# Path attention on one core: where the transposed inverses lie, how much of a level is multiplied, and when the softmax of a batch is done

## The reference, cut to what matters

```python
Mw  = where(strict, einsum('bhtd,bhsd->bhts', wh, wh) * beta, 0)
rhs = where(strict, einsum('bhtd,bhjd->bhtj', wh, kh) * beta, 0)
Bmat = solve_triangular(Mw + eye(t), rhs, lower=True)
qw  = where(incl, einsum('bhid,bhtd->bhit', qh, wh), 0)
logits = (qk - einsum('bhit,bhtj->bhij', qw, Bmat)) * SCALE
p = softmax(where(incl, logits, -1e30)); o = einsum('bhij,bhjd->bhid', p, vh); y = o @ o_w.T
```

## Time and profile before

| | |
|---|---|
| median of 3 runs | 3011.29 us (3009.99 to 3013.78) |
| the profiled execution's own time | 3016.45 us |
| its span, first to last instruction | 3014.4 us |
| TensorE busy | 2675.2 us (89%) |
| VectorE busy | 1644.3 us (55%) |
| ScalarE busy | 974.1 us (32%) |
| GpSimd busy | 742.3 us (25%) |
| path attention, whole | from about 2019 us to about 2801 us of the span |

### The profile page before, as it was taken

One profiled execution on the slowest core, in us unless ns is written; L12 is line 12 of the kernel. 1 busy time (PEld: TensorE's weight loads), 2 busy tenths in 40 slices (PEclk: granted clock), 3 DMA queues, 4 the chain that ended last, 5 costly groups with the idle time before them and its releaser, 6 DMA issues. The chain is left out here.

```text
span 3014.4 us, 84666 instructions
## 1 busy us (share of the span) xinstructions
PE 2675.2 (89%) x37720; PEld 1969.5 (65%) x37720; DVE 1644.3 (55%) x2820; ACT 974.1 (32%) x1590; POOL 742.3 (25%) x951
## 2 busy tenths in 40 slices
PE   5999999999998979988888887779599999998598
PEld 2666766766766545545555554544489988988487
DVE  4344344444442454569999984736666666664500
ACT  2233333333333211145555543116122222222121
POOL 6910000000000000013332324012456656653200
PEclk9899999999999889999999988889799999999699
DMA  2010010010000001132222301000000000000131
GB/s 66 18 35 19 19 35 19 19 35 18 21 17 23 0 27 37 45 97 71 78 88 67 100 17 49 0 17 18 2 4 4 4 3 4 4 4 3 56 140 42
DMA packets 24554, 99.72 MB, mean 33 GB/s; under 512 B 4824, under 2 KB 9837, under 8 KB 19502
## 3 DMA queue, kind: packets, MB, share of 16 engines
q1 hardware_dynamic: 24238, 94.83, 10.8%
HBM read 93.77 MB, written 1.05 MB: 31 GB/s over the span
## 5 line engine op out<-in xcount | busy, mean ns | idle before, releaser
L528 ACT ACTIVATE xa_probT<-psum,zero_column 128x1024 f32<-128x1024 f32 (+1 forms) x224 | 223.8, 1050 | 281.3 <-PE psum L376 281.3
L611 DVE COPY xa_v<-psum 128x512 f32<-128x512 f32 x96 | 66.4, 692 | 426.2 <-PE psum L353 426.2
L2016 POOL TENSOR_TENSOR pa_cT<-pa_mt,pa_levelT_compact 128x256 f32<-128x256 f32 x320 | 234.9, 762 | 167.3 <-DVE pa_mt L2265 116.1
L600 DVE TENSOR_REDUCE xa_part_max<-psum 128x2 f32<-128x802 f32 (+1 forms) x256 | 241.9, 987 | 60.1 <-PE psum L363 60.1
L353 PE MATMUL psum<-xa_wv,xa_ctxT 96*128 96x256 f32 (+1 forms) x832 | 215.4, 402 | 4.6 <-DVE xa_v L611 3.9
L374 PE MATMUL psum<-xa_qbd,xa_kT 32*128 32x128 f32 (+1 forms) x3328 | 219.2, 300 | 0.2
L2146 PE MATMUL psum<-pa_x,pa_inv_invT 64*64 64x64 f32 x3072 | 207.1, 220 | 13.0 <-DVE pa_inv_invT L2319 12.0
L345 PE MATMUL psum<-xa_ctxT,xa_wk 96*128 96x401 f32 (+1 forms) x512 | 209.1, 531 | 3.4 <-ACT xa_kT L521 1.4
L376 PE MATMUL psum<-xa_shift,xa_shift_of 32*128 32x128 f32 (+1 forms) x3328 | 209.1, 271 | 0.0
L1276 POOL TENSOR_TENSOR tk_exp_all<-tk_exp_all,tk_exp_left 128x577 f32<-128x577 f32 x64 | 121.0, 1891 | 354.7 <-ACT tk_exp_left L1397 354.7
L2146 PEld LDWEIGHTS psum<-pa_x,pa_inv_invT 64*64 64x64 f32 x3072 | 195.2, 136 | 19.3 <-issue 16.1
(11 more groups left out here) (482 smaller groups left out, 5286.9 us busy)
## 6 DMA issues: line engine op xcount, KB each, us to landing
tk_ctx<-in_ctx SPq DMA_DIRECT2D x16, 1248.0 KB, 5.3
xa_ctxT<-in_ctxT SPq DMA_DIRECT2D x16, 1200.8 KB, 7.5
tk_ctxT<-in_ctxT SPq DMA_DIRECT2D x16, 1200.8 KB
ec_w<-in_ec_w SPq DMA_DIRECT2D x16, 1024.0 KB, 6.8
m_gate_up<-in_m_gate_up SPq DMA_DIRECT2D x17, 256.0 KB, 2.6
m_down<-in_m_down SPq DMA_DIRECT2D x17, 128.0 KB, 2.4
ff_w<-in_ff_w SPq DMA_DIRECT2D x2, 1024.0 KB
x_resident<-in_x SPq DMA_DIRECT2D x1, 1024.0 KB, 4.9
```

The source lines that it names most:

```text
L528: a_.activation(probT[0:w, par, u, :, 0:n], ps[0:w, at:at + 2, 0:n], ACT.Exp, bias=core.zero[0:w, :]).then_inc(e_done, 1)
L600: v.tensor_reduce(part_max[:, n, m, 2 * u:2 * u + 2], ps[:, at:at + 2, 0:z - a], AX.X, ALU.max, negate=True).then_inc(max_step, 1)
L2016: g_.tensor_tensor(cT[:, (NL * b + n) % 2, g], mt[:, g], four(level_c[:, n, :]), ALU.mult).then_inc(level_ready, 1)
```

## The change

It rewrites the second block of path attention:

- `wt` and `wbt` get a third part (parity 0, 1, 0). With parts 0:2 the product puts even heads in the low half of the partitions, with parts 1:3 in the other. `mt` and `inv` keep their half; `invT` and `rhs` are made on the other one. The old product of 128 moving columns becomes two of 64 with different stationary operands, and q a third one, `queries`, later.
- A product of two 64x64 matrices then goes across the halves or stays, by its operands. `x`, `first`, `z` and `second` go across, the last level's update and the logits stay, and the four products of an `update` (both updates, both halves) are issued one of each in turn: low to high, low to low, high to low, high to high.
- Of each level only the half of the columns that can change is multiplied, copied, masked and subtracted: 32 moving columns where there were 64. Each level has its own `cT` and `x` tile, whose other half is zeroed once.
- POOL masks a level for two or four groups in one instruction; the mask of `rhs` moves from DVE to POOL, after a copy by ACT; ACT also resets the inverses' other halves (`reset`, eight instructions).
- The softmax is two batches late on TensorE: `maxima` and `shift` of b-1 stand on DVE between the next batch's first masks and `sol`, `exponentials` behind the copies of `z`, and `turn_probs` (in two parts), `weigh` and `turn_out` of b-2 between products of batch b, all in bank 7. After the loop the last two batches' softmax alternates with the eight parts of the projection.
- DVE does `log_out(b)` and `masked_q(b+1)` by turns, after `masked_inv(b+1)`.

The core of the diff:

```diff
-        cT = sb("cT", [P, 2, G, 4, T])
-        invs, x = sb("inv_invT", [P, 2, G, 2, 4, T]), sb("x", [P, G, 4, T])
-        wt, wbt, qt = (sb(n, [P, G, 2, T]) for n in ("wt", "wbt", "qt"))
+        cTs = [sb(f"cT{n}", [P, G, 4, T]) for n in range(len(LEVELS))]
+        wt, wbt, qt = sb("wt", [P, G, 3, T]), sb("wbt", [P, G, 3, T]), sb("qt", [P, G, 2, T])
-        y, z = sb("y", [P, G, 4, T]), sb("z", [P, G, 4, T])
+        z = sb("z", [P, G, 4, T // 2])
-        prob = sb("prob", [P, 16, T])
+        prob = sb("prob", [P, 2, 16, T])
...
+            x_bank = lambda n, g: (4, 5, 6, 7)[g] if n == 0 else (4, 0, 2, 6)[g]
+            u_bank = lambda n, g: (4, 0, 2, 6)[g] if n == 0 else (4, 0, 2, 5)[g]
...
                 def begin(b):
+                    for h in range(2):
+                        pool.wait_ge(mt_sb, G * b + 2 * h + 2)
+                        level(b, 0, 2 * h, 2)
+                    transposed_inverse(b)
+
+                def rest(b):
+                    level(b, 1, 0, G)
+                    for h in range(2):
+                        pool.wait_ge(inv_masked, G * b + 2 * h + 2)
+                        add_identity(b, 2 * h, 0, inv_start)
+                    level(b, 2, 0, G)
+                    level(b, 3, 0, G)
                     if b < B - 1:
                         spread_w(b + 1)
+                    pool.wait_ge(rhs_raw, G * b + G)
+                    r = rhs[:].rearrange("p g j c -> p (g j) c")
+                    g_.tensor_tensor(r, r, below[:].unsqueeze(1).broadcast_to([P, 4 * G, T]), ALU.mult).then_inc(rhs_sb, 1)
+                    spread_q(b)
+                    level(b, 4, 0, G)
...
+                def wb_products(g):
+                    return [(g * P, wt[:, g, 0:2], wb[:, g], alone), (g * P + T, wt[:, g, 1:3], wb[:, g], alone)]
+
+                def q_products(g):
+                    return [(4 * T + g * T, wt[:, g, 0:2], q[:, g], alone)]
+
+                def right_products(g):
+                    return [(g * P, wbt[:, g, 0:2], w[:, g], alone), (g * P + T, wbt[:, g, 1:3], k[:, g], alone)]
...
+                def right_sides(b):
+                    pe.wait_ge(w_spread, 2 * b + 2)
+                    if b:
+                        pe.wait_ge(sol_sb, G * b)
+                    strips(4, right_products, b, mr_ps)
...
+                def product(bank, col, left, right, g, out_cross):
+                    for j in range(4):
+                        for a in range(2):
+                            rows, out = half[a], half[a ^ out_cross]
+                            l, r = left(rows, j), right(rows, j)
+                            o_ = ps[out, bank, col + 32 * j:col + 32 * j + 32]
...
+                            mm = mmul(o_, l, r, start=True, stop=True)
+                    return mm
...
+                def x_product(b, n, g):
+                    s = LEVELS[n]
+                    pe.wait_ge(level_ready, leveled(b, n, g))
+                    if n == 0:
+
+                        pe.wait_ge(inv_start, 2 * b + g // 2 + 1)
+                        pe.wait_ge(rhs_raw, G * b + g + 1)
+                    else:
+                        pe.wait_ge(t_done, G * (NI * b + n - 1) + g + 1)
+                    c = flatter(cTs[n][:, g])
+                    product(x_bank(n, g), 0, of(c), halved(inverse(b, g, 0), s, 0), g, 1).then_inc(x_ps, 1)
...
+                    for j in range(4):
+                        for a, which in ((1, 0), (1, 1), (0, 0), (0, 1)):
+                            rows = half[a]
+                            left, right = ((of(invT), halved(x, s, 0)), (of(x), halved(invT, s, 1)))[which]
+                            mm = mmul(spot(high if which else low, half[a ^ 1 ^ which], j), left(rows, j), right(rows, j),
+                                      start=True, stop=True)
+                    mm.then_inc(t_ps, 1)
...
                 def batch(b):
                     for n in range(NI):
+                        for g in range(G):
+                            x_product(b, n, g)
+                        if n in (1, 2) and b >= 2:
+                            attend[2 * n - 2](b - 2)
                         for g in range(G):
                             update(b, n, g)
+                        if n in (1, 3) and b >= 2:
+                            attend[n](b - 2)
                     if b < B - 1:
+                        first_matrices(b + 1)
+                    for step in (first, z_product, second):
+                        for g in range(G):
+                            step(b, g)
                     if b < B - 1:
+                        queries(b + 1)
+                    raw_logits(b)
+                    if b < B - 1:
+                        right_sides(b + 1)
+                    for g in range(G):
+                        logits(b, g)
...
                 for t in range(TILES):
+                    attend[t % 4](B - 2 + t // 4)
+                    if t == 0:
+                        pe.wait_ge(ot_sb, KD * (B - 2))
+                    project(t)
...
+                def reset(b):
...
+                    for which in range(2):
+                        one = part(ident_c[:], 1, 1 - which).rearrange("p n s -> p (n s)")
+                        for g in range(G):
+                            ins_ = a.activation(m[:, g, which, :, :, 1 - which], four(one), ACT.Copy)
+                        ins_.then_inc(inv_reset, 1)
+
+                def right_out(b):
+                    for g in range(G):
+                        act.wait_ge(inv_masked, G * b + g + 1)
+                        a.activation(rhs[:, g], kind(4 + g, 1), ACT.Copy).then_inc(rhs_raw, 1)
...
+                            m = both_inverses(b, g, s)
+                            v.tensor_tensor(m, m, ps[:, u_bank(n, g):u_bank(n, g) + 2, 2 * T:4 * T].rearrange("p k (n s) -> p k n s", s=s),
                                             ALU.subtract).then_inc(t_done, 1)
...
                     if b < B - 1:
+                        masked_wb(b + 1)
+                    if b:
+                        maxima(b - 1)
+                        shift(b - 1)
                     for g in range(G):
+                        dve.wait_ge(w_ps, G * b + g + 1)
+                        m = sol[:, g, :, 0:T // 2]
+                        v.tensor_tensor(m, m, ps[:, 4 + g, 6 * T:8 * T].rearrange("p (j c) -> p j c", j=4),
+                                        ALU.subtract).then_inc(sol_sb, 1)
+                    if b < B - 1:
+                        for g in range(G):
+                            masked_inv(b + 1, g)
                     for g in range(G):
                         log_out(b, g)
+                        if b < B - 1:
+                            masked_q(b + 1, g)
+                    if b:
+                        sums(b - 1)
```

More of the change, by code:

```diff
@@ L1792, in _ @@
                 same_blocks(16, blocks[:])
+                for m in cTs + xs:
+                    c.step(g.memset(m[:], 0.0))
                 g.memset(same[:], 0.0).then_inc(masks, 1)
@@ L2019, in begin @@
-                def begin(b):
[L2020 to L2036, removed]
+                        pool.wait_ge(q_ps, G * b)
+                    spread(wt, w[:, :, cols_of(b)], 3).then_inc(w_spread, 1)
+                    spread(wbt, wb[:, :, cols_of(b)], 3).then_inc(w_spread, 1)
+                def spread_q(b):
+                    if b:
+                        pool.wait_ge(log_ps, G * b)
+                    spread(qt, q[:, :, cols_of(b)], 2).then_inc(q_spread, 1)
@@ new lines, in add_identity, with transposed_inverse @@
+                def add_identity(b, g0, which, done):
+                    at = (b % 2 * G + g0) * 8 * T
+                    m = invs[:, at:at + 16 * T].rearrange("p (g k j n two) -> p g k j n two", g=2, k=2, j=4, two=2)
+                    for g in range(2):
+                        i = m[:, g, which, :, :, which]
+                        ins_ = g_.tensor_tensor(i, i, four(part(ident_c[:], 1, which).rearrange("p n s -> p (n s)")), ALU.add)
+                    ins_.then_inc(done, 1)
+                def transposed_inverse(b):
+                    for h in range(2):
+                        pool.wait_ge(invT_masked, G * b + 2 * h + 2)
+                        add_identity(b, 2 * h, 1, invT_start)
@@ L2056, in _, with strips @@
                 mmul = nc.tensor.matmul
-                def strips(at, left, right, b, done):
+                def strips(at, products, b, done):
                     for g in range(G):
[L2061 to L2066, removed]
@@ new lines, in first @@
+                def first(b, g):
+                    if g == 0:
+                        pe.wait_ge(t_done, G * NI * (b + 1))
+                        pe.wait_ge(rhs_sb, b + 1)
+                        if b >= 2:
+                            pe.wait_ge(ot_sb, KD * (b - 1))
+                    invT = inverse(b, g, 1)
+                    for j in range(4):
+                        for a in range(2):
```

(21 more changed lines are left out.)

405 lines of the change are left out of this document (211 added, 194 removed).

## The result

The kernel after takes **3131.47 us** (median of 4 runs, 3118.11 to 3140.43) against 3010.64 for the kernel before, run beside it: ratio 1.0408, interval 1.0351 to 1.0464. It is slower by 4%, where I forecast 3% faster. The profiled execution took 3139.03 us, its span is 3137.3.

What follows compares the result with a forecast made beforehand. TensorE was taken to bound the sixteen path-attention batches; -4.1 us a batch times 16 = -66, then -17, -3.7, -7.4 and +3 gave -91 us, so 2920 us; range 2885 to 2995, about 8 in 10.

Steps and rivals of the forecast that it cites:

- (a): Updates on four tiles instead of two: 1.97 instead of 3.94 us a level, three levels, -5.9 us a batch.
- rival 1: Updates: tiles that share rows exclude each other, so their gain is 0; +94, 3015 us, no change; 8%.
- (b): Strips: each product of 128 moving columns becomes two of 64, 96 instructions more at 27 ns, +2.6 us a batch.
- (c): Half of the columns in x, the last update, z and second: 0 a batch, lower bound -1.7 us.
- (d): Softmax parts on TensorE: one more switch of shape and one back, +0.2 us a batch.
- (e): Waits that go: strips for sol, x of level 3 for the divided output, logits' pair waits; -1.5 us a batch.
- (f): Waits that come at the batch boundary, near misses on POOL's identities and VectorE: +0.5 us a batch, bounds 0 and 4.
- rival 3: Batch boundary becomes a wait, POOL perhaps half as fast on the new shapes: +64, 2985 us; 14%.
- Rival 2: x, first, z, second, logits: two row tiles in one PSUM bank wait for each other; +242, about 3160 us; 8%.
- (g): Four long runs of shift, held up while POOL masks, cost 20 us; most of that goes, -17 us.
- (h): Ends of the block: -3.7 for one batch's softmax fewer in the loop, -7.4 at the end, +3 at the start.
- the forecast's 34 us: Sign that the forecast holds: a batch of path attention takes 34 us, where it took 38.75.

Runs made afterwards that it cites:

- fewer: `whole` without three quarters of the third level's updates (heads j 1 to 3 left out), 192 TensorE instructions fewer a batch: 2932.36 us, ratio 0.9741.
- whole: Kernel of after with all 64 columns moved again in x, the updates and the last update; z and second stay at half: 2969.86 us, ratio 0.9859.
- whole_x: Kernel of after with all 64 columns moved in the x products alone; the updates move 32: 2968.91 us, ratio 0.9863.
- whole_two: `whole` with an update's matmuls issued in another order, the four heads of inv first, then those of invT: 2960.64 us, ratio 0.9843.
- inter: `whole` with x products and updates alternating inside a level, updates' PSUM banks moved, three more waits for VectorE's subtractions: 2958.38 us, ratio 0.9837.
- again: `whole` with the third level's updates issued twice, 256 instructions more in each batch: 3028.02 us, ratio 1.0067.

## Why the prediction was wrong

The rivals were all about waits and tiles, none about the clock, and the range ended at 2995: the cause lay outside of everything I had listed.

- **(a) Updates on four tiles: right in the array, lost twice, to the clock and then to the supply of instructions.** 1.92 to 2.2 us a level at the upper clock, for 1.97. So the rule of the Trainium skill's page "TensorE: Matmul & The Clock Gate" (Part 3, The mechanism), that a weight load overlaps only when the row group differs (rival 1), does not hold here: of four tiles two share each row group, and 128 instructions took 1.92 us.
- **(b) Strips: right in pace, wrong in price.** 27.4 ns each. But in a kernel bound by supply 96 matmuls more, with their weight loads, cost by the runs above 192 / 256 of 3.6 to 3.9 us, 2.7 to 2.9, whatever their pace (an estimate; `fewer` got 2.3 for leaving 192 out); I had 2.6 by the array's pace, the same size by chance.
- **(c) Half of the columns: the step that failed.** I wrote "fewer moving columns buy nearly nothing" and set it to 0 a batch, bounded by a gain alone, -1.7; for the updates, which were halved too, I priced nothing. The pace was right (28.3 ns). Left out was that it can cost: with the columns halved at the same pace the granted clock fell to 0.69. The price of the halves in `x`, the updates and the last update is after less `whole`, **162 us**, 10 a batch. `x` made whole alone returns 163 of it, the updates and the last update alone 153, so it is no sum of two prices: either is enough. A row of before could have warned me: the clock of the tail's stretch is 0.78, so it was not a constant of the kernel.
- **(d), (e), (f), rival 3: right as far as seen.** The wait for `sol` is gone, and none for POOL's identities came. POOL's identity adds take 0.63 us each where I had 0.5, and TensorE is seen to wait for none.
- **Rival 2: refuted.** Both halves of a product write one PSUM bank in `z`, at 28.3 ns. The Trainium skill's page "TensorEngine Tiling (Array Packing)" (Gotcha 1: PSUM Pressure) says otherwise; the trace decides.
- **(g) The long `shift`: right.** Its maximum is 1.61 us (its median rose from 1.26 to 1.6), and in `whole` no batch has the 5 us more that some had before.
- **(h) Ends: right at the end; the +3 at the start did not come.** From the end of the last logits to the end of the projection `whole` takes 20.6 us (2745.25 to 2765.84), forecast 22.1, before 29.5. From the last raw logits to the end of the span it is 2981.2 - 2743.0 = 238.2 us in `whole` and 3014.4 - 2769.1 = 245.3 before: -7.1 for -7.4. The first raw logits come 13.3 us later than before in `whole`, but the block itself starts 14.7 us later there: its first strips start at 2140.5 us before, 2155.2 in `whole`, 2138.4 in `whole_x`, 2157.2 after. From there to the first raw logits it is 43.1 us before, 41.7 in `whole` and 41.0 in `whole_x`, so -1.4 and -2.1 for +3; after has 49.5, at the lower clock. The lines are those of the instructions of the raw logits, first and last start at the end; before, `whole`, `whole_x`, after:

```profile
L2083 PE MATMUL psum<-pa_w_k,pa_qt x512: 217/270/318, 2183.6 to 2769.1; 32*128 32x64 f32 x171
```

```profile
L2148 PE MATMUL psum<-pa_w_k,pa_qt x512: 270/270/318, 2196.9 to 2743.0; 32*128 32x64 f32 x171
```

```profile
L2148 PE MATMUL psum<-pa_w_k,pa_qt x512: 270/270/318, 2179.4 to 2730.9; 32*128 32x64 f32 x171
```

```profile
L2148 PE MATMUL psum<-pa_w_k,pa_qt x512: 270/270/468, 2206.7 to 2900.7; 32*128 32x64 f32 x171
```

The late start comes from linear attention, a thousand us earlier, which the change doesn't touch. Its last L738 starts at 1078.9 us before and 1095.7 after; `whole` and `whole_x` have the same code up to there, and yet (L738, then 1035 to 1090 us, first `whole`, then `whole_x`):

```profile
L738 PE MATMUL psum<-la_bo,ones_row x16: 626/708/791, 1000.1 to 1097.0; 1*128 1x256 f32 x16
...
L738 PE MATMUL psum<-la_bo,ones_row x16: 374/554/791, 997.8 to 1077.5; 1*128 1x256 f32 x16
```

```profile
1035.00:1090.00 55.00, 45.22 (x136) 26.24 (x136) 23.66 (x44) 5.87 (x11) 0.62 (x1) 0.62 0.00 0
...
1035.00:1090.00 55.00, 38.53 (x165) 24.06 (x164) 29.97 (x70) 10.48 (x18) 0.19 (x2) 0.77 0.05 15
```

The granted clock of the same instructions was 0.62 in one execution and 0.77 in the other, and it ends some 20 us later in the first. So two executions are compared by stretches of the changed block, not by their spans.
- **The sum.** Between the marks of the raw logits it is 585.5 us before, 546.1 in `whole`, 694.0 after. These are fifteen batches, which at the forecast's 34 us would be 510. The 34 us needed the array's pace; supply makes the batch 36.2 to 36.4, which is the 36 us between 546.1 and 510 and most of the 50 between `whole` and the forecast. The rest is not accounted for.

## What to carry to other kernels

Before small matmuls are made smaller, read what sets their pace: where fewer moving columns leave it as it is, they save nothing and can take the upper clock away, so give TensorE the whole columns and let the other engines read the half they need. And count instructions beside the array's pace: more tiles at a time pay only until the instruction queue's packets (here one of 16 KB each 3.9 us, 256 instructions) set the mean; from there an instruction left out was worth 12 ns here and one put in cost 14, though by the array's pace (128 updates with their weight loads in 1.92 us) it would be 7.5. By this reading a faster array is worth nothing there; no run made it faster. When clock and pace are both in play, run the change once with its work made whole again: that separated the two here in one run.

## What the runs showed of the hardware that was not expected

- TensorE was busy 707.6 of 740 us in after and yet at the lower clock for some 0.6 of the time ((1 - 0.69) / 0.5). Halving the moving columns of two thirds of the matmuls (704 of 1076), with the copies and subtractions behind them, took the kernel before from 0.99 to 0.80. Whether it is their number or their lying in strips is open.
- The same instructions in linear attention had a granted clock of 0.62 in one execution and 0.77 in another, and ended 20 us apart.
- Instructions have a rate. Over 500 us the mean was never above one packet of 16 KB in 3.9 us (`whole`, `whole_two`, `inter`, `again`), and no two packets started less than 3.2 us apart; where the array would need them faster, "issue" waits of up to 2.1 us appear inside groups. The Trainium skill's page "Runtime: NRT & Kernel Launch" (Instruction fetch mechanics) gives the same blocks of 16 KiB or 256 instructions, and calls the cost of crossing one "mostly hidden"; at four tiles a time the trace does not agree.
- Matmuls on different pairs of tiles are seen in turn though they were issued in blocks, so the order in the code does not settle which tiles are in use together: a level of updates in that order took 2.74 us, neither 3.94 nor 2.1. At the upper clock it hardly changed the time (2960.64 us and 2969.86), with halves it did (3076.86 and 3131.47).
- Two row tiles in one PSUM bank do not wait for each other: `z` writes both halves of a bank at 28.3 ns an instruction.
